# Cross-attention block with a ternary FFN on one core: weight steps moved to batches 1 to 6, and two row pairs of the second FFN group moved into the last attention slots

## The reference

```python
n = layernorm(x)
s = causal_mask((n @ w_q) @ (ctx @ w_k).T / sqrt(512))          # per batch, 1024 x 1024
x = x + tanh(g_xattn) * softmax(s) @ (ctx @ w_v)
def ternary(w): return clip(round(w / mean(abs(w))), -1, 1)     # in value
h = gelu(layernorm(x) @ ternary(W1).T + b1)                     # 512 -> 2048
out = x + tanh(g_ffn) * (h @ ternary(W2).T + b2)                # 2048 -> 512
```

## Time and profile before

| what | value |
|---|---|
| median of 3 runs | 1618.36 us (1613.87 to 1619.16) |
| span of the profiled execution | 1614.5 us |
| attention, from slot 2 of batch 1 to the last scores | 157.35 to 757.11 us |
| FFN units | from 757.11 us to the end |
| PE busy | 1574.7 us, 98% of the span |
| DVE, ACT, POOL busy | 67%, 50%, 30% of the span |

### The profile page before, as it was taken

One profiled execution on the slowest core, in us unless ns is written; L12 is line 12 of the kernel. 1 busy time (PEld: TensorE's weight loads), 2 busy tenths in 40 slices (PEclk: granted clock), 3 DMA queues, 4 the chain that ended last, 5 costly groups with the idle time before them and its releaser, 6 DMA issues.

```text
span 1614.5 us, 26067 instructions
## 1 busy us (share of the span) xinstructions
PE 1574.7 (98%) x10028; PEld 982.1 (61%) x10028; DVE 1087.3 (67%) x1825; ACT 811.1 (50%) x1448; POOL 481.5 (30%) x467
## 2 busy tenths in 40 slices
PE   7799999999999999999989999999999999999998
PEld 4455556565656555555656666666666666666665
DVE  6666657665656679866666677667676677667664
ACT  2333333433233553323656666666666666666664
POOL 3211111111111111133344443345344444345320
PEclk9899999999999999999999999999999999999999
DMA  7445455453646986666222333324222323323110
GB/s 209 111 94 150 104 142 111 113 133 91 153 101 169 222 249 158 150 156 119 63 76 48 97 79 85 78 55 98 76 76 47 98 76 82 74 65 98 50 50 27
DMA packets 307532, 170.81 MB, mean 106 GB/s; under 512 B 268160, under 2 KB 268176, under 8 KB 306128
## 3 DMA queue, kind: packets, MB, share of 16 engines
q1 hardware_dynamic: 306512, 166.78, 42.2%
q10 hardware_dynamic: 720, 2.10, 0.4%
q0 software_dynamic: 176, 0.27, 0.1%
HBM read 70.53 MB, written 33.55 MB: 64 GB/s over the span
## 4 chain that ended last, share of the span: by engine, by line
PE 89%; DVE 4%; issue 2%; ACT 1%; DMA 1%; POOL 0%; SPq 0%; DVEq 0%
PE s_ps L1234 14%; PE e_ps L1234 14%; PE s_ps L1299 11%; PE o_ps L1329 10%; PE v_ps L1280 9%; PE t_ps L1261 8%; PE t_ps L1178 7%; PE o_ps L1178 7%; PE v_ps L1178 7%; PE m_ps L1178 3%; DVE w_s L1074 1%; DMA x_ring<-in_x 1%; DVE negmax L897 0%; PE e_ps L1329 0%; DVE ctx_s L742 0%
## 5 line engine op out<-in xcount | busy, mean ns | idle before, releaser
L1037 DVE SCALAR_TENSOR_TENSOR v_s<-xnT,sc,v_s 128x512 f16<-128x512 f32 x256 | 239.7, 957 | 104.7 <-ACT v_s L667 104.7
L660 ACT ACTIVATE xnT<-tT,b_s 128x256 f32<-128x256 f32 x384 | 173.9, 499 | 178.5 <-DVE tT L1025 62.2
L1234 PE MATMUL s_ps<-w_s,v_s 128*128 128x512 f16 x1024 | 262.8, 379 | 0.0
L1234 PE MATMUL e_ps<-w_s,v_s 128*128 128x512 f16 x1024 | 262.8, 379 | 0.0
L563 ACT ACTIVATE p<-s_ps,ebias,esc 128x128 f32<-128x128 f32 (+3 forms) x64 | 53.2, 831 | 355.7 <-DVE ebias L901 355.7
L1299 PE MATMUL s_ps<-ctx_s,tT 128*128 128x512 f16 (+3 forms) x1152 | 197.7, 326 | 3.7 <-DVE tT L858 3.7
L1329 PE MATMUL o_ps<-v_s,pT 128*128 128x512 f16 x840 | 192.0, 380 | 0.0
L1280 PE MATMUL v_ps<-wv_s,ctx_s 128*128 128x512 f16 x768 | 180.0, 385 | 7.8 <-DVE v_s L865 7.8
L1261 PE MATMUL t_ps<-xnT,a_s 128*128 128x256 f16 x1488 | 176.9, 276 | 8.2 <-issue 7.9
L667 ACT ACTIVATE v_s<-xnT,sc 128x512 f16<-128x512 f32 x256 | 176.2, 712 | 7.5
L1234 PEld LDWEIGHTS e_ps<-w_s,v_s 128*128 128x128 f16 x1024 | 100.2, 98 | 120.8
(11 more groups left out here) (169 smaller groups left out, 2401.5 us busy)
## 6 DMA issues: line engine op xcount, KB each, us to landing
out_y<-x_ring SPq DMA_DIRECT2D x128, 256.0 KB, 2.2
x_ring<-in_x SPq DMA_DIRECT2D x64, 256.0 KB, 3.0
raw<-in_ctxT SPq DMA_DIRECT2D x7, 2048.0 KB, 8.2
raw<-out_y SPq DMA_DIRECT2D x44, 256.0 KB, 3.8
w_in<-in_w1T SPq DMA_DIRECT2D x16, 512.0 KB, 4.3
w_in<-in_w2T SPq DMA_DIRECT2D x16, 512.0 KB, 4.4
x_ring<-out_y SPq DMA_DIRECT2D x20, 256.0 KB, 3.7
raw<-in_ctxT SPq DMA_DIRECT2D x2, 1024.0 KB, 16.3
```

Source lines behind the costliest of these rows:

```text
L660: a.activation(g32n[:, j, half * 2 * P:(half + 1) * 2 * P], src, ACT.Gelu, bias=b1_s[:, f:f + 1], scale=1.0 / YN).then_inc(g_act, 1)
L1037: v.scalar_tensor_tensor(out=g_s[:, U % 2, j, LO], in0=g32n[:, j], scalar=col(C_SG), in1=g_s[:, U % 2, j, HI], op0=ALU.mult, op1=ALU.subtr ...
L1234: last_mm = mm(y_ps[i], g_s[:, U % 2, j, a, i * P:(i + 1) * P], w2_s[:, f, :], start=(U % UG == 0 and n == 0 and a == HI), stop=(U % UG == ...
```

## The change

Three things change. The S steps go to slots 8 to 15 (W1) and 17 to 24 (W2), one in each; the T steps go to positions 4, 5, 6 and 8 of batches 3 to 6, that is slots 28, 29, 30, 32, 36, 37, 38, 40, 44, 45, 46, 48, 52, 53, 54 and 56; the totals are taken in slots 16 and 25. The first six rows of the FFN (`EARLY = 6`: group 0 and pair 2 of group 1) are made in slots 57 to 62 and pair 2's `y_upper` and `y_lower` in slot 63; pair 3 moves from unit 1 to unit 0. And `y_normal` in a slot moves from before the T step and line 865 to the slot's end, behind line 951 and the context work. Pair 2's rows go to buffers of their own: the first 2048 elements of `w_in`, with a wait for all T steps, and `xn32` and `xn_s` laid side by side, with a wait for the transposes that read them.

```diff
+        xn_both = sb("xn_both", [P, 2, 2, D])
+        xn32 = xn_both[:, 0]
...
-        W_PLAN = {NT - 22: "SS", NT - 21: "SS", NT - 20: "SS", NT - 19: "SS", NT - 18: "TSS", NT - 17: "TSS",
-                  NT - 16: "TSS", NT - 15: "TSS", **{NT - n: "T" for n in range(14, 2, -1)}}
-        TOTAL_SLOTS = {NT - 19: 0, NT - 15: 1}
+        W_PLAN = {**{t: "S" for t in range(TB, 2 * TB)}, **{t: "S" for t in range(2 * TB + 1, 3 * TB + 1)},
+                  **{b * TB + n: "T" for b in range(3, 7) for n in (4, 5, 6, 8)}}
+        TOTAL_SLOTS = {2 * TB: 0, 3 * TB + 1: 1}
...
-            n = 0 if q < 2 else 1 + q % 2
+            n = 0 if q < 2 else 3 if q == 2 else 1 + q % 2
...
-        ROWS_Q0 = {rows_step(g): g for g in range(1, NG)}
-        ROWS_Q1 = {rows_step(g) + 1: g for g in range(1, NG)}
+        EARLY = 6
+        ROWS_Q0 = {rows_step(g): g for g in range(2, NG)}
+        ROWS_Q1 = {0: 1, **{rows_step(g) + 1: g for g in range(2, NG)}}
...  (POOL)
-                if last and 0 <= e < GT:
+                if last and 0 <= e < EARLY:
...
-                if last and e in (2, 4):
+                if last and e in (2, 4, 6):
                     y_lower(e // 2 - 1)
...  (ACT)
-                if last and t in (FIRST_Y + 2, FIRST_Y + 4):
+                if last and t in (FIRST_Y + 2, FIRST_Y + 4, FIRST_Y + 6):
                     y_upper((t - FIRST_Y) // 2 - 1)
...
+                if q == 2:
+                    for i in range(2):
+                        act.wait_ge(x_turned[i], 16 * NT)
...  (DVE)
-                y_row = t - FIRST_Y if last and FIRST_Y <= t < FIRST_Y + GT else None
+                y_row = t - FIRST_Y if last and FIRST_Y <= t < FIRST_Y + EARLY else None
...
-                if y_row is not None:
-                    y_normal(y_row)
                 for m, n in terns[:1]:
                     ternary(m, n)
...
                     for q in CTX_SPLITS.get(c, ()):
                         ctx_lower(batch, (s // TB + 1) % 2, q)
+                if y_row is not None:
+                    y_normal(y_row)
...
+                if q == 2:
+                    dve.wait_ge(w_ternary, NW)
```

More of the change, by code:

```diff
@@ L65, in gated_block @@
         x_ring = sb("x_ring", [P, 8, D])
-        xn32 = sb("xn32", [P, 2, D])
-        xn_s = sb("xn_s", [P, 2, 2, D], F16)
+        xn_both = sb("xn_both", [P, 2, 2, D])
+        xn32 = xn_both[:, 0]
+        xn_s = xn_both[:, 1].rearrange("p r d -> p (r d)").bitcast(F16).rearrange("p (r a d) -> p r a d", r=2, a=2)
         p32 = sb("p32", [P, S])
@@ L120, in gated_block @@
         rows8 = [flat.bitcast(F32).rearrange("p (o n) -> p o n", o=8)
-                 for flat in (v_old[:, 0:4096], pT[:, :].rearrange("p r a j n -> p (r a j n)"), v_new[:, 0:4096])]
+                 for flat in (v_old[:, 0:4096], pT[:, :].rearrange("p r a j n -> p (r a j n)"), v_new[:, 0:4096],
+                              w_in[:, :, :].rearrange("p r n -> p (r n)")[:, 0:2048].bitcast(F16))]
         rows7 = [flat.rearrange("p (a o n) -> p a o n", a=2, o=7)
                  for flat in (v_old[:, 4096:7680], p_s[:, :].rearrange("p r a n -> p (r a n)")[:, 0:3584],
-                              v_new[:, 4096:7680])]
+                              v_new[:, 4096:7680],
+                              xn_both[:, :, :, :].rearrange("p w r d -> p (w r d)").bitcast(F16)[:, 0:3584])]
         y_out = x_ring[:, 0:4]
```

## The result

The changed kernel takes 1601.61 us (median of 4 runs, 1600.03 to 1602.30) against 1616.11 us for the kernel before (4 runs, 1613.34 to 1619.16). The ratio is 0.9909, with a 95% interval of 0.9896 to 0.9921. The profiled execution took 1601.66 us with a span of 1599.9 us, 14.6 us shorter than the span of before.

What follows compares the result with a forecast made beforehand. It took the PE as the bound, busy 1574.7 of 1614.5 us, with losses in three places. Terms 5.0 + 5.3 + 9.4 = 19.7 us, so 1618.4 - 19.7 = 1598.7 us, range 1593 to 1602, chance 0.70.

Steps and rivals of the forecast that it cites:

- Slots 49 to 51, 5.0 us: Batch from slot 50: with no T at positions 1, 2, 3, 7 and at most one load a slot, 5.0 us go.
- slots 59 and 60, 5.3 us: Slots 59 and 60: with line 865 before y_normal and no T step there, the 5.3 us lost go.
- The late y_normal: Slot 60: its mask comes about 1.3 us late behind y_normal; wide cover before the softmax is needed, so cost nothing.
- rival 3: Slots 60 and 61: the late y_normal holds the softmax, the 5.3 us stay elsewhere, 1604 us; chance 0.06.
- Unit 4, 9.4 us: FFN unit 4: pair 3, made in unit 0, lands 6.1 us before unit 4 asks for it; all 9.4 us go.
- rivals 2 and 5: Unit 4 still waits: pair 3 held up (2) or something new keeps pair 2 late (5); 1608 us; chance 0.09 together.
- The moved steps, 0: S and T steps in their new slots, and one load at five batch ends, cost the PE nothing: 0 us.
- rival 1: Position 1 of five batches: weight loads at batch ends delay the x tile; 1604 us, at worst 1614; chance 0.10.
- rival 4: All 16 T-step slots: T collides with POOL's line 444, delaying line 865; 1635 us, collision alone 1615; chance 0.05.
- What is late next is nothing that I can see: After unit 4's wait goes: no new wait expected, only the 4.1 us of the FFN's tail.
- the path of pair 2 in slot 63: Slot 63: sums, y_upper, y_lower (3.6 us) and transpose (6.2) done by 776, some 25 us before pair 3.
- the wider range: Whole kernel: 1593 to 1609 us, the forecast together with rivals 1 to 3 (rival 1 at its third).

Runs made afterwards that it cites:

- order_only: The kernel before with only y_normal moved to the slot's end: 1610.05 us, ratio 0.9960.
- plan_only: The kernel before with only the new W_PLAN and TOTAL_SLOTS: 1606.17 us, ratio 0.9939.
- t_short: The kernel of lower_later with the T steps at positions 1, 2, 3 and 7 of batches 3 to 6 instead of 4, 5, 6 and 8: 1606.72 us.
- load_bunch: The kernel of lower_later with the last three S steps together in slot 24, so three weight loads go out in slot 23: 1597.43 us, one run.
- lower_later: The changed kernel with POOL's y_lower(2) moved from slot 63 to behind last_sum(0) in unit 0: 1595.73 us, ratio 0.9876.
- lower_half: The changed kernel with y_lower(2) cut in two, 3 of 7 rows in slot 63 and 4 behind last_sum(0): 1598.91 us, one run.

## Why the prediction was right in sign and range, and where its sum failed

*Slots 49 to 51, 5.0 us, and slots 59 and 60, 5.3 us.* Both terms came: -10.2 us measured for -10.3. The reason given for slots 59 and 60 holds (order_only), and it was more than needed (plan_only). The reason for slots 49 to 51 named two causes together. t_short shows one of them by itself, 2.4 us a batch; the loads alone at one batch end did nothing (load_bunch).

*The late y_normal.* Worked out as a mask about 1.3 us late, at no cost. In the kernel after, DVE stands 3.18 us for `y_lower(0)`, and the mask of slot 60 starts directly behind it at 710.80, 1.3 us after the scores end (706.13 + 3.42 = 709.55). The PE waits for nothing there, and rival 3 falls:

```profile
706.13 3.42 PE L1308 MATMUL s_ps<-ctx_s,tT 128*128 128x512 f16 x24
710.34 0.55 DVE L1020 TENSOR_SCALAR v_s<-raw,mv,rstd 128x512 f32<-128x512 f32 x1 [3.18 <-POOL v_s L486]
710.80 0.29 DVE L902 TENSOR_TENSOR s_ps<-s_ps,causal 128x128 f32<-128x128 f32 x1
```

*Unit 4, 9.4 us.* It came in full, and rivals 2 and 5 fall. The transposes of pairs 2 and 3 are now issued at 773.02 and 794.89; with 6.2 us to land, pair 3 is there at 801.1, and unit 4 starts at 807.68, 6.6 us later, without a pause. Pair 2 lands near 779, not by 776, which costs nothing:

```profile
773.02 5.62 SPq L340 DMA_TRANSPOSE ctx_s<-xn_both  x1
794.89 4.17 SPq L340 DMA_TRANSPOSE ctx_s<-v_s  x1
```

*The moved steps, 0.* Right: no wait of the PE from 70 to 751 us. DVE's line 913 (906 of before) never waits for an x tile, so rival 1 falls too. All T steps run beside POOL's line 448 (444 of before), 2.28 us at the median as in the earlier trace rows, and rival 4 has no case.

```profile
L1083 DVE SCALAR_TENSOR_TENSOR w_s<-w_in,sc,g x16: 2056/2279/2286, 361.6 to 676.0; 128x1024 f16<-128x1024 f32 x16
```

One row was misread in the prediction: the 70.19 us "without a T" (slots 44 to 49) have T steps in slots 46 to 48. The batch from 423.18 us, which has none, gives the same for slots 36 to 41, 511.79 - 441.60 = 70.19, so the conclusion stands.

```profile
441.60 3.26 PE s_ps L1299 x24
```

*The step that failed* is in the part on unit 4: "What is late next is nothing that I can see", and before it the path of pair 2 in slot 63, where POOL's `y_lower` stood as 3.6 us of a path with time to spare. I asked when its result would be there, and bounded ACT's `y_upper` ahead of the first gelu (0, as taken, by lower_later). I did not ask what runs on DVE in those 3.6 us. It is `weight_sums`, whose third and fourth sums the PE was already waiting for in the kernel before (0.56 us): no cover at all. Price: 3.3 us more waiting and 2.8 us at the lower clock. The rule of the Trainium skill that I cited for the T steps, in "SBUF — State Buffer", section "Who interferes with whom", covers this pair as well: a `tensor_tensor` with both inputs in SBUF is named there as contending with GpSimd's reads. The runs agree (3.34 us of delay for 3.58 us on POOL, 1.40 for 1.64). I applied it where the cost was hidden, and not to the one POOL instruction that the change added beside work on the critical path.

With these 6.2 us the forecast would have been 1598.7 + 6.2 = 1604.9 us. Two differences that have nothing to do with the change bring it down to the measured 1601.6: 1.2 us of a quicker start, and 1.8 us outside the span instead of 3.9. (The 3.9 set the median of three runs against the span of one; wherever both are known for one execution, the time is 1.8 us above the span.) That the time lies inside the forecast's own range, 1593 to 1602, is therefore luck; the sign and the wider range did not need it.

## What to carry to other kernels

When an instruction of POOL is moved, look up which DVE instructions with two operands in SBUF fall into its time, not only who waits for its result: DVE's delay was nearly POOL's whole length where both started together, and it costs what the DVE instruction's own cover does not hold. Two edits that each remove the same wait give their gain once. And a DVE step is free or not by its slot: 6 us were hidden in slots of 11 to 14 us but for two short waits, 3 us were not in slots of 7 and 8.5.

## What the runs showed of the hardware

A DVE instruction with two SBUF inputs and a POOL `tensor_tensor` that started within 0.11 us of each other: DVE's took longer by nearly POOL's length, 1.0 us for 1.16 (T steps, POOL starting 0.04 us behind DVE), 1.40 for 1.64 and 3.34 for 3.58 (DVE starting 0.10 and 0.11 us behind POOL). POOL was not slowed there (3.57 us in lower_later, 3.58 beside DVE's pair). Kernel after, a T step and POOL beside it:

```profile
373.35 2.28 DVE L1083 SCALAR_TENSOR_TENSOR w_s<-w_in,sc,g 128x1024 f16<-128x1024 f32 x1
373.39 1.16 POOL L448 TENSOR_TENSOR xn_both<-xn_both 128x512 f16<-128x512 f32 x1 [3.15 <-ACT xn_both L590]
```

It can be POOL that waits. In the FFN of the kernel before, DVE's `y_lower` (line 1044) starts 0.15 us ahead of POOL's line 471 and takes 2.01 us, and POOL's instruction takes 2.44 us instead of the 0.73 it takes without DVE beside it; so it is in all 15 such pairs of the trace:

```profile
798.52 2.01 DVE L1044 TENSOR_TENSOR p_s<-pT,p_s 128x1792 f16<-128x1792 f32 x1
798.67 2.44 POOL L471 TENSOR_TENSOR v_s<-v_s 128x256 f32<-128x256 f32 x1 [1.09 <-DVE v_s L1011]
```

After waits of 1.95 us (lower_half) and 1.65 us the PE's products ran at full length, at a granted clock of 1.00. After 2.08 us (order_only), 2.23 us, 3.89 us (kernel after) and 7.47 us the next ones were up to twice as long: the granted clock over them was 0.62, 0.67, 0.50 and 0.60, where 0.50 is the level of 1.2 GHz and 1.00 that of 2.4. The wait of 3.89 us cost 2.8 us on top of itself.
